# First batch's text tiles normed ahead of its image tile, the other batches' embedding in two halves, decay by heads

## The reference

```python
p = patches of 16x16x3                       # 36 per image, 768 values each
h = concatenate([p @ W.T + b, txt], axis=1)  # (8, 548, 192)
n = layernorm(h)
q, k, v = n @ Wq.T, n @ Wk.T, n @ Wv.T       # 3 heads of 64
scores = (q . k) / 8 * decay                 # decay = gamma ** (m - l) for m >= l, else 0
o = softmax(scores) . v                      # a masked score is 0 and takes part in the softmax
o = (o - mean) / sqrt(var + eps)             # per batch and head, over tokens and width
h = h + (o * gn_weight + gn_bias) @ Wo.T
n = layernorm(h)
comb = softmax(n @ router_w.T), top 8 of 16 kept, made to sum to 1
out = h + sum over experts of comb[e] * (gelu(n @ w1[e]) @ w2[e])   # 8 of width 128, 8 of width 256
```

## Time and profile before

| what | us |
|---|---|
| median of 3 runs (lowest, highest) | 764.25 (762.29, 764.98) |
| profiled execution, own time | 762.86 |
| its span | 761.1 |
| PE busy | 720.0 (95%) |
| DVE busy | 574.0 (75%) |
| ACT busy | 469.9 (62%) |
| POOL busy | 158.5 (21%) |
| mean granted TensorE clock | 0.993 of full speed |

### The profile page before, as it was taken

The page is one execution under the profiler, slowest core; times in us unless marked ns, Lnnn a source line. Parts: engine busy times, 40 slices in busy tenths (PEclk is TensorE's granted clock), DMA queues, the critical chain, the costliest instruction groups (busy, mean ns, idle before and its releaser), DMA issues.

```text
span 761.1 us, 13144 instructions
## 1 busy us (share of the span) xinstructions
PE 720.0 (95%) x4265; PEld 605.9 (80%) x4265; DVE 574.0 (75%) x1584; ACT 469.9 (62%) x1049; POOL 158.5 (21%) x278
## 2 busy tenths in 40 slices
PE   5978999999998979999999999999999999999996
PEld 4767888888887757888888888888888888888895
DVE  6899888988887657677777777777777777677675
ACT  2678788788787726456456456456456456456453
POOL 3062564574541980000000000000000000000000
PEclk9999999999999989999999999999999999999998
DMA  6700011012112361455255255255265355254142
GB/s 196 210 23 5 20 44 44 3 44 54 55 44 66 125 201 32 113 132 127 77 132 133 71 136 126 74 136 129 70 131 127 76 135 123 71 132 93 47 86 43
DMA packets 120565, 70.14 MB, mean 92 GB/s; under 512 B 82000, under 2 KB 100496, under 8 KB 120496
## 3 DMA queue, kind: packets, MB, share of 16 engines
q1 hardware_dynamic: 120496, 69.31, 36.2%
HBM read 58.65 MB, written 10.63 MB: 91 GB/s over the span
## 4 chain that ended last, share of the span: by engine, by line
PE 77%; ACT 9%; DVE 7%; issue 2%; POOL 1%; DMA 1%; POOLq 1%; DVEq 1%; SPq 1%
PE ps L1425 75%; ACT pt L684 3%; ACT ot L684 2%; ACT pr L764 1%; DVE pr L1117 1%; PE ps L1574 1%; DMA pat<-patches 1%; ACT k_hi L684 1%; DVE sc L1095 1%; DVE xb L1058 1%; ACT xa_hi L684 1%; DVE xa_lo L1058 1%; ACT q L684 0%; DMA gate<-comb_dram 0%; POOL w_lo L641 0%
## 5 line engine op out<-in xcount | busy, mean ns | idle before, releaser
L904 ACT ACTIVATE act<-ps 128x512 f32<-128x512 f32 (+1 forms) x216 | 124.9, 579 | 194.0 <-PE ps L1425 192.7
L1318 DVE TENSOR_TENSOR act<-act,gate 128x512 f32<-128x512 f32 (+1 forms) x216 | 145.5, 674 | 127.3 <-ACT act L904 112.1
L1425 PE MATMUL ps<-x,w_hi 128*128 128x512 f32 (+1 forms) x648 | 215.9, 389 | 0.9 <-ACT act L904 0.8
L1425 PE MATMUL ps<-x,w_lo 128*128 128x512 f32 (+1 forms) x432 | 165.5, 383 | 0.0
L1058 DVE TENSOR_TENSOR act_lo<-act,act_hi 128x512 fp32r<-128x512 f32 (+1 forms) x216 | 145.1, 672 | 0.2
L1425 PEld LDWEIGHTS ps<-x,w_hi 128*128 128x128 f32 x648 | 121.0, 189 | 26.4 <-ACT act L904 2.0
L684 ACT ACTIVATE act_hi<-act 128x512 fp32r<-128x512 f32 (+1 forms) x216 | 130.2, 603 | 9.5 <-DVE act L1318 9.3
L1425 PEld LDWEIGHTS ps<-x,w_lo 128*128 128x128 f32 x432 | 81.5, 189 | 16.4
L1425 PE MATMUL ps<-act_hi,w_hi 128*128 128x512 f32 (+1 forms) x216 | 83.2, 385 | 7.4 <-DVE act_lo L1058 7.3
L536 POOL TENSOR_TENSOR rstdb<-vepsb,neg_half 128x4 f32<-128x4 f32 x9 | 9.7, 1073 | 372.6 <-DVE vepsb L1181 372.6
L1425 PE MATMUL ps<-act_lo,w_hi 128*128 128x512 f32 (+1 forms) x216 | 83.5, 387 | 0.0
(11 more groups left out here) (183 smaller groups left out, 1201.2 us busy)
## 6 DMA issues: line engine op xcount, KB each, us to landing
gate<-comb_dram SPq DMA_DIRECT2D x128, 256.0 KB, 3.6
w_raw<-w SPq DMA_DIRECT2D x16, 384.0 KB, 3.7
h_dram<-h SPq DMA_DIRECT2D x8, 384.0 KB
res<-h_dram SPq DMA_DIRECT2D x8, 384.0 KB, 4.1
rb<-h_dram SPq DMA_DIRECT2D x48, 64.0 KB, 2.6
out<-rb SPq DMA_DIRECT2D x48, 64.0 KB, 1.9
x_dram<-xn_t SPq DMA_DIRECT2D x24, 96.0 KB, 2.4
gate<-comb_dram SPq DMA_DIRECT2D x16, 144.0 KB, 3.0
```

What stands on the lines that cost most here:

```text
L904: a.activation(act[j % 3][:, 0:n], ps[:, up_bank(j), 0:n], ACT.Gelu_apprx_tanh).then_inc(gelu_done, 1)
L1318: dve.tensor_tensor(act[j % 3][:, 0:n], act[j % 3][:, 0:n], gate[e % 4][:, 0:n], ALU.mult).then_inc(gated, 1)
L1425: return pe.matmul(dst, w, x, start=start, stop=stop)
```

## The change

VectorE doubles the decay vectors from 128 to 256 before the statistics and from 256 on after the normalising. The text tiles' variances go to GpSimd ahead of tile 0's, with semaphores of their own, and GpSimd makes scale and shift in two passes. ScalarE normalises tiles 1 to 4, VectorE tile 0 and the repeated columns. TensorE turns the four text tiles before tile 0. Part 0 of the other batches' embedding runs as three steps behind these transposes and three behind the first projection; ScalarE copies it out after the fourth rounding of q and k. `weights_hi(1)` goes behind `x_hi`, `round_router` between the first exponentials. The decay goes out and back by heads, and `apply_decay` waits per head. At the start of the feed-forward part, gates 5 to 7 and 8 to 9 and 10 to 11 are issued in groups, and GpSimd splits part 2 before it norms the second tile. The image's turned tokens use bank 3 rather than 2.

```diff
 WO_BANKS = (2, 3, 7)
 GN_BANK = 3
 IMG_REST = 5
-IMG_BANKS = (2, 5, 2, 7, 3)
+IMG_BANKS = (3, 5, 2, 7, 3)
 TILE_ORDER = (0, 1, 4, 2, 3)
 LAST_X2 = (1, 7)
...
         ld_aw, ld_pat, ld_gam, ld_gn = [sem("ld_aw0"), sem("ld_aw1")], [sem("ld_pat0"), sem("ld_pat1"), sem("ld_pat2")], sem("ld_gam"), sem("ld_gn")
         ld_h0, ld_h1, ld_h = sem("ld_h0"), sem("ld_h1"), sem("ld_h")
         consts = sem("consts")
-        decay_built, decay_stored, ld_decay = sem("decay_built"), sem("decay_stored"), sem("ld_decay")
+        decay_built = sem("decay_built")
+        decay_stored, ld_decay = [sem(f"decay_stored{i}") for i in range(H)], [sem(f"ld_decay{i}") for i in range(H)]
+        text_var, text_rstd, image_normed = sem("text_var"), sem("text_rstd"), sem("image_normed")
         aw_hi_ready, aw_lo_ready = sem("aw_hi_ready"), sem("aw_lo_ready")
         emb_done, emb_copied, embt_done, embt_copied = sem("emb_done"), sem("emb_copied"), sem("embt_done"), sem("embt_copied")
...
             sp.dma_start(gnb[:, :], gn_b).then_inc(ld_gn, 16)
             sp.wait_ge(decay_built, 1)
-            sp.dma_start(decay_rows.rearrange("h (p l) -> p h l", l=DECAY_L), drow[:, :, :]).then_inc(decay_stored, 16)
-            sp.wait_ge(decay_stored, 16)
+            for hh in range(H):
+                sp.dma_start(decay_rows[hh:hh + 1, :].rearrange("h (p l) -> p h l", l=DECAY_L),
+                             drow[:, hh:hh + 1, :]).then_inc(decay_stored[hh], 16)
             shifted = decay_rows[:, 127:127 + P * (DECAY_L - 1)].rearrange("h (p l) -> p h l", l=DECAY_L - 1)
-            sp.dma_start(decay[:, :, :], shifted[:, :, 0:L]).then_inc(ld_decay, 16)
+            for hh in range(H):
+                sp.wait_ge(decay_stored[hh], 16)
+                sp.dma_start(decay[:, hh:hh + 1, :], shifted[:, hh:hh + 1, 0:L]).then_inc(ld_decay[hh], 16)
             load_h(1, 2, ld_h1)
             sp.dma_start(w1_raw, w1[:, :, 0:W1_SHARE]).then_inc(ld_w1, 16)
             load_h(2, B, ld_h)
...
             load_w2(2)
             gates(0, 4, 5)
             load_w2(3)
-            gates(0, 5, 6)
+            gates(0, 5, 8)
             load_w2(4)
-            gates(0, 6, 7)
+            gates(0, 8, 10)
             load_w2(5)
-            gates(0, 7, 8)
+            gates(0, 10, 12)
             load_w2(6)
-            gates(0, 8, 9)
             load_w2(7)
-            gates(0, 9, 12)
             store_h(LB - 1)
             gates(0, 12, 15)
             store_h(LB)
...
                     pool.wait_ge(aw_lo_ready, 2)
                     pool.wait_ge(embt_copied, 5)
-                    pool.wait_ge(ld_decay, 16)
+                    for hh in range(H):
+                        pool.wait_ge(ld_decay[hh], 16)
                 cols = bass.ds(b * W1_SHARE, W1_SHARE)
                 for c in range(2):
                     pool.tensor_copy(w1_hi[:, c, cols], w1_raw[:, c, :])
...
                     last = pool.tensor_tensor(w1_lo[:, c, cols], w1_raw[:, c, :], w1_hi[:, c, cols], ALU.subtract)
                 last.then_inc(w1_split, 1)
-            rstd_of(0, ln1_var, rstd, mv, veps, nmr, ln1_rstd)
+            def first_rstd(cols, var, ready):
+                pool.wait_ge(var, 1)
+                apart(pool, "pool")
+                pool.tensor_tensor(rstd[:, cols], veps[:, cols], neg_half[:, cols], ALU.pow)
+                pool.tensor_tensor(nmr[:, cols], zeros[:, cols], mv[:, cols, 0], ALU.subtract)
+                pool.drain()
+                pool.tensor_tensor(nmr[:, cols], nmr[:, cols], rstd[:, cols], ALU.mult).then_inc(ready, 1)
+                pool.drain()
+
+            first_rstd(slice(1, NT), text_var, text_rstd)
+            first_rstd(slice(0, 1), ln1_var, ln1_rstd)
             pool.wait_ge(ld_gn, 32)
             def gn_coefficients(t):
...
             gn_coefficients(LB - 1)
             split_w2(0)
             split_w2(1)
+            split_w2(2)
             second_rstd(1)
             pool.drain()
             pool.wait_ge(x2t_done, 2)
             norm_second()
-            for p in range(2, W2_PARTS - 1):
+            for p in range(3, W2_PARTS - 1):
                 split_w2(p)
             gn_coefficients(LB)
             split_w2(W2_PARTS - 1)
...
                 qk_round(b, 3)
                 if tail:
                     pt_copy(t, 2)
+                if not tail:
+                    a.wait_ge(emb_done, 2)
+                    embedded(emb[:, 0, IMG:B * IMG], ps[:, 0, 0:(B - 1) * IMG], 0).then_inc(emb_copied, 1)
                 a.wait_ge(qk_hi, nth(b, 5, 4))
                 copy(k2_hi[0:HD, :], k2_hi[HD:P, :]).then_inc(qk_hi, 1)
                 if not more:
                     second_norm(0)
                 exps(b, 0, (0, 1))
                 if not tail:
+                    round_router()
                     a.wait_ge(emb_done, 3)
                     embedded(emb[0:HD, 1, IMG:B * IMG], ps[0:HD, IMG_REST, 0:(B - 1) * IMG], 1).then_inc(emb_copied, 1)
                 exps(b, 0, (2, 3, 4))
...
                     o_copy(b, 1, LAST_O[1])
                     gn_totals(t, LAST_GN[t])
-            norm_apply(0, rstd, nmr, ln1_rstd, xn, first_normed, range(DVE_TILES, NT))
-            weights_hi(1)
+            norm_apply(0, rstd, nmr, text_rstd, xn, first_normed, range(1, NT))
             x_hi(0, 0)
             x_hi(0, 1)
-            a.wait_ge(emb_done, 2)
-            embedded(emb[:, 0, IMG:B * IMG], ps[:, 0, 0:(B - 1) * IMG], 0).then_inc(emb_copied, 1)
-            round_router()
+            weights_hi(1)
             iterations(body)
             def gelu(j):
...
                 dve.drain()
                 dve.tensor_scalar(ve[:, :], m2[:, :, 1], EPS, None, ALU.add).then_inc(signal, 1)
-            def norm_share(b, rs, nmean, rs_ready, dst, normed):
-
-                dve.wait_ge(rs_ready, nth(b, 1, 1))
-                for I in range(NT):
-                    r = rows(I)
-                    for at, f0 in ((0, 0), (D, P)):
-                        if at or I < DVE_TILES:
-                            last = dve.tensor_scalar(dst[:r, I, at:at + D - f0], tokens(h, b, I)[:, f0:D],
-                                                     rs[:r, I:I + 1], nmean[:r, I:I + 1], ALU.mult, ALU.add)
-                last.then_inc(normed, 1)
-
             def image_tokens(i):
                 dve.wait_ge(embt_done, i + 1)
...
                 src = ps[0:IMG, IMG_BANKS[i], 0:n * D].rearrange("p (b d) -> p b d", b=n)
                 dve.tensor_copy(h[0:IMG, b0:b0 + n, 0, :], src).then_inc(embt_copied, 1)
+            decay_powers(128, 256)
             dve.wait_ge(ld_h0, 16 * NT)
             norm_parts(0, st6, range(1, NT))
-            decay_powers(128, 256)
+            dve.drain()
+            for I in range(1, NT):
+                dve.bn_aggr(mv[:rows(I), I, :], st6[:rows(I), I, :])
+            dve.drain()
+            dve.tensor_scalar(veps[:, 1:NT], mv[:, 1:NT, 1], EPS, None, ALU.add).then_inc(text_var, 1)
             image_tokens(0)
             dve.drain()
             norm_parts(0, st6, (0,))
             dve.drain()
-            norm_join(st6, mv, veps, ln1_var)
+            dve.bn_aggr(mv[:, 0, :], st6[:, 0, :])
+            dve.drain()
+            dve.tensor_scalar(veps[:, 0:1], mv[:, 0:1, 1], EPS, None, ALU.add).then_inc(ln1_var, 1)
+
+            def normed_part(I, f0, at):
+                r = rows(I)
+                return dve.tensor_scalar(xn[:r, I, at:at + D - f0], tokens(h, 0, I)[:, f0:D], rstd[:r, I:I + 1], nmr[:r, I:I + 1],
+                                         ALU.mult, ALU.add)
+
+            dve.wait_ge(text_rstd, 1)
+            for I in range(1, NT):
+                last = normed_part(I, P, D)
+            last.then_inc(first_normed, 1)
+            dve.wait_ge(ln1_rstd, 1)
+            normed_part(0, 0, 0)
+            normed_part(0, P, D).then_inc(image_normed, 1)
             decay_powers(256, L - 1).then_inc(decay_built, 1)
-            norm_share(0, rstd, nmr, ln1_rstd, xn, first_normed)
             weights_lo(0)
             for t in (0, 1):
                 dve.memset(mx[t][:, :], 0.0)
...
             def apply_decay(b, hh):
                 s = hh % 2
+                if b == 0:
+                    dve.wait_ge(ld_decay[hh], 16)
                 for I in TILE_ORDER:
                     r, n = rows(I), L - P * I
                     if hh != 1 and I in (0, 2):
...
                     second_part(0, 0)
                     second_part(0, 1)
                 if b == 0:
-                    dve.wait_ge(ld_decay, 16)
                     dve.wait_ge(consts, 3)
                 apply_decay(b, 0)
                 apply_decay(b, 1)
...
                 return last
-            def embed(part, bank, n0, n1):
+            def embed(part, bank, n0, n1, ks=range(KT)):
                 f0, f1 = ((0, P), (P, D))[part]
-                for k in range(KT):
+                for k in ks:
                     if n0 == 0 and part == 0 and k in (0, KT // 2):
```

(23 more changed lines are left out.)

## The result

The changed kernel takes **765.89 us** (median of 13 runs, 764.38 to 766.6), the kernel before 762.58 in 13 runs of the same session (761.82 to 764.98): ratio 1.0034, 95% interval 1.0026 to 1.0043, slower. The forecast was no change at 763.8. The measured 765.89 lies inside the range 760.6 to 767.0 only because that range starts from 764.25, the median of three runs, and thirteen runs of the same kernel give 762.58: against its own base the forecast was -0.45 and the result +3.3. The profiled execution of after took 765.32 (span 763.5), that of before 762.86 (span 761.1).

What follows compares the result with a forecast made beforehand. Bounds: the head's serial chain and TensorE's 6.24 us stall on expert 6's gate, 8.2 with the slow clock. Head +1.05 and feed-forward -1.5 sum to -0.45: 763.8 us against the median 764.25, range 760.6 to 767.0.

Steps and rivals of the forecast that it cites:

- The feed-forward term (-1.5): Feed-forward start: of 8.2 us of stall and slow clock removed, 1.5 stays gained, as TensorE then waits for GpSimd's coefficients.
- scales and normalising took 5.75: Feed-forward start, GpSimd: this work was kept at its old 5.75 us in the new order, ending at 266.15.
- The end of the coefficients, 282.7: Feed-forward start, GpSimd: the last batch's coefficients end at 282.7, behind split 6, with ScalarE waiting from 277.3.
- GpSimd falls behind: Slower rival, feed-forward start: each split takes 4.27 beside busy VectorE, coefficients end at 286.7, 767.8 us; chance 0.15.
- moved only: Rival, feed-forward start: coefficients at 284.2, nothing gained there, 764.25 + 1.05 = 765.3 us; chance 0.13.
- the early end: Feed-forward start: with all of GpSimd's splits undisturbed, the coefficients come at 277.5.
- the head's bounds: Head: between +0.3 and +2.4 us, giving the forecast a range of 762.8 to 765.2.
- The head term (+1.05): Head: first division by the softmax's sums starts 1.05 us later, and the delay is passed on.
- the 0.7 us at the sums: Head: VectorE is free for the sums at 17.55 against 18.27, a gain of 0.7 us.
- the open half of the embedding: Head, between projections and scores: six matmuls take 1.3 us, ScalarE's copy 0.46; scores start at 25.8.
- First division near 33.4: Head: a sign that the forecast is right, beside sums at 17.5 and scores near 25.8.
- The one-column power: Head, GpSimd: the image tile's power takes 0.6 us; above 0.7 would be a sign against the forecast.

Runs made afterwards that it cites:

- before_again: The kernel before, unchanged, run once more for a second trace: 763.49 us, one run.
- ff_only: The kernel before with both new feed-forward orders (gates grouped, part 2 split ahead of the norming): 762.54 us, ratio 1.0000.
- gates_only: The kernel before with the gates grouped alone, GpSimd's order as it was: 761.32 us, ratio 0.9982.
- decay_whole: The changed kernel with one store and one load for all three decay tables, as before: 764.84 us, ratio 1.0032.
- head_only: The changed kernel with SyncE's and GpSimd's feed-forward orders put back, leaving the new head: 766.69 us, ratio 1.0046.
- coeff_early: The changed kernel with the last batch's coefficients made after part 3 is split, not after part 6: 759.41 us, ratio 0.9956.
- embed_ahead: The changed kernel with all twelve embedding matmuls between the transposes and the first projection, copied out in ScalarE's old place: 764.74 us, ratio 1.0024.
- norm_only: The changed kernel with the whole embedding ahead of the transposes, as in before; new norming, transposes and decay stay: 764.06 us, ratio 1.0019.
- gates_coeff: The kernel before with the gates grouped and the coefficients made after part 3 is split, part 2 left behind the norming: 756.06 us, ratio 0.9905.
- late: The kernel before with a 1500-column memset on VectorE between the first sums and the first remainder: 765.72 us, ratio 1.0036.
- gates_coeff_patches: `gates_coeff` with the patches' load issued one place earlier: 757.26 us, ratio 0.9925.

## Why the prediction was wrong

**The feed-forward term (-1.5) failed at one step**, "scales and normalising took 5.75", kept at that price in a new place, beside other work of VectorE. The direction of the chain was right: the gate is no releaser any more, the stall moves to ScalarE's `y_round` behind `gshift`, 5 to 6 us long, and the clock falls after it. The end of the coefficients, 282.7 in the forecast and 286.57 in after, splits up as follows. Split 2 ended at 262.04 instead of 260.4: 1.6 late, by the head and the clock (below), at 4.02 us where 4.27 was taken. Scales and normalising took 9.27 (262.04 to 271.31) instead of 5.75: 3.5 late. The four splits behind them, with 1.01 of waiting for a load, took 12.46 instead of 13.55, and the coefficients 2.8 instead of 3.0: 1.3 early. So the one bad term is the norming, 6.23 for four pieces that take 2.07 in before. Counted from the totals of LB-1, `gshift` starts 38.8 us later in after and 36.8 later in before: 2.0 us, which is the difference between the forecast -1.5 and the measured +0.5 (515.4 to 515.9).

Why they are slow is seen in what VectorE does beside them. The four pieces in before (GpSimd's timeline), and under them VectorE's beside them (to 261.07):

```profile
259.00 2.07 POOL L564 TENSOR_SCALAR xn<-res,rstdb,nmrb 128x192 f32<-128x192 f32 x4 [0.32 <-issue]
```

```profile
259.14 0.78 DVE L1123 BATCH_NORM_STATS2 gst<-ot 64x6 f32<-64x274 f32 x2
259.99 0.27 DVE L1132 BATCH_NORM_AGGREGATE gmv<-gst 128x2 f32<-128x12 f32 x2
260.34 0.25 DVE L1134 TENSOR_TENSOR gtmp<-gmv 128x2 f32<-128x2 f32 x1
260.66 0.41 DVE L1136 TENSOR_TENSOR gmv<-gmv,gtmp 128x2 f32<-128x2 f32 x1
```

And in after, beside the same four (264.34 to 270.57):

```profile
264.09 0.69 DVE L1343 TENSOR_TENSOR act<-act,gate 128x512 f32<-128x512 f32 x1
264.70 0.68 DVE L1082 TENSOR_TENSOR act_lo<-act,act_hi 128x512 fp32r<-128x512 f32 x1
265.30 0.72 DVE L1082 TENSOR_TENSOR y<-ot,y 128x548 fp32r<-128x548 f32 x1
265.94 0.83 DVE L1343 TENSOR_TENSOR act<-act,gate 128x512 f32<-128x512 f32 x1
...
268.27 0.88 DVE L1343 TENSOR_TENSOR act<-act,gate 128x512 f32<-128x512 f32 x1
```

VectorE is busy in both (1.93 and 1.85 of 2 us in before's windows 258 to 262, 1.97 to 2.00 in after's 264 to 270). What differs is the kind of work: statistics of one input there, an unbroken row of large operations on two inputs from SBUF here. The Trainium skill (SBUF — State Buffer, "Who interferes with whom") says that a VectorE instruction with two SBUF inputs and a GpSimd one that reads SBUF shut each other out, and that one with at most one SBUF input, outside its two-port modes, does not. The traces agree, and the prediction weighed the rule for the splits alone. The norming pieces felt it most, 0.52 to a mean of 1.56 each, and some of VectorE's operations went from 0.68 to 0.83 and 0.88.

The kernel before shows the same by itself. In its second trace (`before_again`) the pieces start 1.0 us earlier against VectorE's row, meet two of its two-input operations before the statistics, and take 2.94. GpSimd's and VectorE's timelines:

```profile
258.01 2.94 POOL L564 TENSOR_SCALAR xn<-res,rstdb,nmrb 128x192 f32<-128x192 f32 x4 [0.32 <-issue]
```

```profile
257.92 0.67 DVE L1318 TENSOR_TENSOR act<-act,gate 128x512 f32<-128x512 f32 x1
258.51 0.68 DVE L1058 TENSOR_TENSOR act_lo<-act,act_hi 128x512 fp32r<-128x512 f32 x1
```

So 2.07 was itself the lower of two values. All eight traces with split 2 behind the norming have 2.06 to 2.08 or 2.92 to 2.94, all six with it ahead 6.23 to 6.25, and `ff_only` against `gates_only` (6.24 and 2.93) is that one edit. That the place is the cause is shown by this; that it acts through VectorE's two-input operations rests on the timelines laid side by side, since no run held the rest still and changed VectorE's work alone.

The rival *GpSimd falls behind* named the right engine, but put the delay into the splits and priced it at 4.0. The rival *moved only*, nothing gained here and the head's loss kept, describes this part best: 286.57 less the 1.9 by which after is late at the totals is 284.7, and it took 284.2. That its 765.3 also lies nearest to the measured time is in part luck, since it is 1.05 over a base that was 1.7 too high. Two of the text's bounds do not follow from its terms: with 2.82 for undisturbed coefficients (246.05 to 248.87) the early end is 277.9, not 277.5, and the head's bounds around 763.8 give 763.05 to 765.15, not 762.8 to 765.2; nothing hangs on either.

**The head term (+1.05) had the right chain and the wrong size.** The profiled pair shows +1.16 at the first division, so the steps were right for that pair. Over many executions the loss ahead of the totals is larger, for two reasons.

First, the 0.7 us at the sums was read from one execution. The old head's sums wait for the patches to land, and over its eight traces (two of them with the patches' load one place earlier) they start anywhere from 16.79 to 19.24, 17.8 on average; before, at 18.27, is late among them. The new head's start at 17.62 to 18.06 in every trace with the embedding behind the transposes, again 17.8 on average: in after they wait for VectorE. So next to nothing is gained there. What is left is the open half of the embedding. From the sums to the first division the old head takes 14.60 us (before, a second trace of it and four variants). The new one takes 16.41 in after, 16.39 in `decay_whole`, and 16.83 and 16.72 in `head_only` and `coeff_early`, where TensorE's slow pace lasts into the first projection; `embed_ahead` takes 15.25, `norm_only` 14.79. The price is **1.8 to 2.2 us**, and 1.2 of it comes back when the embedding is not split. By the first division itself, 34.3 on average in those four traces and 32.5 in the five of the old head without an edit to the head, it is 1.8.

Second, the clock. The prediction gave no term to the stretch between 60 and 245 us. The granted clock falls near 241 to 247 in five of six traces with the new head, and in one of eight with the old. The cost is 1.1 us: from the last division to the totals 1.74 or 1.75 in the eight traces without a fall and 2.78 to 2.87 in the six with one (after: 244.77 to 247.61). Each run also reports its mean granted clock, which tells of all the runs, not only of the profiled ones:

| kernel | runs by mean granted clock (mean us) |
|---|---|
| before, beside the experiments | 58 of 67 at 0.993 (762.91), 7 at 0.991 (762.24); one at 0.990, one at 0.987 |
| after | 3 at 0.993 (764.58), 4 at 0.991 (765.70), 6 at 0.989 (766.11) |
| `norm_only` | 7 at 0.993 (763.57), 4 at 0.989 (764.66), 1 at 0.987 |
| `gates_coeff` | 3 at 0.997, 1 at 0.998 |

Three runs of after had before's usual clock, and they took 764.58, 1.8 over before's mean of 762.81: about the price of the open half. The other ten had lost one or two steps of 0.002. A fall of 4 us to about half speed is a step: 4 x 0.45 / 763 = 0.0024. These ten bring the mean to 765.63, another 1.05. So 765.63 - 762.81 = 2.82 us splits into 1.8 and 1.05. The sum closes by its making, since both parts come from the same runs; what speaks for it is that 1.8 agrees with the price of the open half, and the first step, 764.58 to 765.70, with the 1.1 that a fall at 241 costs in the traces.

The clock alone does not tell a run's time, however. Before's seven runs at 0.991 were faster than those at 0.993, and the second step costs only 0.4 in after. A fall can cost little or nothing where it lies: with one at 41 to 45, `head_only` and `coeff_early` take 211.45 and 211.33 from the first to the last division where after takes 210.74 and before 211.09, but `gates_only`, with one at 38 to 42, takes 210.88. The feed-forward half adds nothing, by `ff_only`.

What makes the clock fall oftener with the new head stays **open**. Being later does not (`late`). `embed_ahead` and `norm_only`, with only part of the new head, still show it, less in `norm_only`. In the traces of `late` and `gates_coeff_patches` a fall in the head follows a pause of TensorE of 1.30 and 1.17 us, but such a pause is no sufficient sign: `norm_only` pauses 1.46 at 19.95 without one, and the pause of 1.37 near 39 is followed by a fall in `gates_only` and by none in before. The falls at 241 us have no pause right before them that before lacks.

**Signs named as telling:** sums, scores, the stall's length and its releaser were as foretold. The stall came 17 us after the old one instead of 14, and GpSimd waited 1.01 for split 6's load instead of 0.3. "First division near 33.4" contradicted the text's own +1.05, which gives 33.9; it was 34.03. The decay and text loads were waited for nowhere. The one-column power took 0.58 (0.6 taken). Most of these signs came true while the time went the other way; none of them measured the norming.

## What to carry to other kernels

A step moved on an engine off the critical path must be priced beside its new neighbour, not at the duration that it had beside the old one: norming that took 2.07 us beside statistics took 6.23 beside operations on two inputs. When a wait is removed, move the next late thing in the same edit; the grouped gates alone gave 1.7 us, with the coefficients in front of the later splits 7. And a gain that hangs on when one load lands wants several executions before it is booked: here most of the 0.7 us was the chance of one trace.

## What was unexpected of the hardware

- The start of the sums in the unchanged head varied by 2.45 us between traces (16.79 to 19.24), by when the patches landed and how fast the twelve matmuls behind them ran (4.31 to 5.41).
- The granted clock fell to 0.50 for about 4 us while TensorE was busy, in stretches of small matmuls (after's 241 to 245; `head_only`, `coeff_early`, `norm_only` and, with the old head, `gates_only` also somewhere in 38 to 46), in some executions and not in others of the same kernel.
- In `late` the clock fell after a pause of TensorE of 1.30 us, so that a delay of 1.4 us cost 2.85; in `norm_only` a pause of 1.46 us, at 19.95, was followed by none until 40.
- In the head matmuls ran at half pace in slices where the clock reads full: six of 252 columns took 2.50 at 17.29 and 1.44 at 23.82.
